# Latent attention: the normalised rows of tiles 2 to 15 are turned in 32x32 blocks by VectorE and put in order by DMA through DRAM, instead of by TensorE and ScalarE

## The chip, the cores and the metric

The kernel runs on one core of one Trainium2 chip. The metric is the device time of one execution in microseconds. Engines: PE is TensorE (PEld its weight loads), DVE is VectorE, ACT is ScalarE, POOL is GpSimd, SP is SyncE, which only issues DMAs (SPq is its queue).

## The reference

Two transformer layers over 64 sequences of 32 rows of 256 numbers: each is cross attention, self attention and a feed-forward part. The change lies in the cross attention of the second layer, over 257 context rows of 64 numbers, with 16 heads and keys kept in a latent form:

```python
x = x + _L1_xattn_ref(_layernorm(x, axis=-1), ctx_512, ...)
...
    q_hk = (hidden_q @ Wq.T).reshape(b, s, H, K)
    q_big = jnp.einsum('bshk,hkq->bshq', q_hk, w_kc_q)
    kv_rope = kv_c * cos[None] + _rotate_half(kv_c) * sin[None]
    q_r = jnp.einsum('bshq,hqr->bhsr', q_big, W_qr)
    k_r = jnp.einsum('bld,hdr->bhlr', kv_rope, W_kr)
    scores = jnp.einsum('bhsr,bhlr->bhsl', q_r, k_r)
    attn = jax.nn.softmax(scores, axis=-1)
    ctx_c = jnp.einsum('bhsl,bld->bhsd', attn, kv_rope)
    ctx_lat = jnp.einsum('bhsd,hkd->bshk', ctx_c, w_kc_kv)
    out = ctx_lat.reshape(b, s, H * K) @ Wo.T
```

Everything is in float32. The weights of the first and the last products are folded before this stage, so that one product gives the queries against `kv_rope` (`a_w`) and one gives the output (`b_w`).

## The kernel before

The 2048 rows are 16 tiles of 128 rows; a tile holds 4 sequences (TB) of 32 rows (SEQ). The stage is the function `latent_attention`. Each engine has its own program, and they meet by semaphores that count; every program walks the steps t = -2 to 16 (`run_steps`), and most steps are the two halves of a loop. In step t TensorE works on three tiles at once:

- `scores` of tile t, in 4 groups of 4 heads, each in one of two PSUM tiles `ps_s`, which is free again when ScalarE has taken the exponentials of the group before last in it
- `weigh_slots` and `weigh_tail`: the keys of tile t-1 weighed with its exponentials, and at the end `finish`, its output products
- `queries` of tile t+1 in two halves, from `xnT`, the normalised rows with their 256 columns on the partitions; then `last_key`, the scores of context row 257 of tile t+1
- `turn` of tile t+2: two transposes through PSUM that make `xnT`, which ScalarE copies out in `turned_out`

The order in a step of TensorE is: scores 0, weighing first half, scores 1, weighing second half and tail, scores 2, queries first half, scores 3, queries second half, output products, last key, turn. The first half of the weighing waits until VectorE has turned the last scores (`turn_last`, semaphore `last_ready`) and all exponentials of the tile.

VectorE takes in a step: inverse sums of tile t-1, then for the groups of tile t the maxima and, one group behind, the 32x32 transposes of the exponentials (`turn_exps`); between them it copies the weighed sums out; at the end it adds the residual, turns the last scores of the next tile, and takes the statistics of the finished row. ScalarE takes exponentials 0 and 1, a small copy, exponentials 2, the two copies of the queries (`queries_out`), exponentials 3 and the last exponentials, and then the copy of the turned row. SyncE loads keys (`load_kT`: two DMAs once the scores of tile t-2 are made, for tile t) and the inverse sums. GpSimd normalises the row of tile t+2 or t+3 (`row_normalised`) when the row before it has been turned, and multiplies the weighed sums by the inverses.

```python
                if live(1):
                    last_key(t + 1, 1 - u)
                if live(2):
                    turn(t + 2)
```

The DMAs of this kernel are issued by SyncE and GpSimd; ScalarE issues none.

Of the kernel before, what the change touches and what calls it, by code (L numbers as in the profile page):

```python
# [4 lines left out]
F32 = mybir.dt.float32  # L5
# [7 lines left out]
P = 128  # L13
# [1509 lines left out]
def latent_attention(nc, name, scope, moments, x_sb, consts, ident, latent_keys, last_roped, a_w, b_w, lastT, background=None):  # L1523
# [5 lines left out]
    xn = sb("xn", [P, DIM])  # L1529
    xnT = sb("xnT", [P, KC, P])  # L1530
    qT = [sb(f"qT{u}", [P, TB, pairs, SEQ]) for u in range(2)]
    kT, kv = latent_keys.kT, latent_keys.kv
# [23 lines left out]

    names = ("dve_next taken xn_ready turned xnT_ready q_made q_out cols_ready scores_made raw_top_ready top_ready "
             "exps_ready exps_turned last_made last_ready last_shifted last_exps whole_ready tail_filled tail_ready inverse_stored inverse_in0 inverse_in1 weighed "
# [4 lines left out]
    with nc.Block() as block:  # L1563
# [38 lines left out]
        def _(pool):  # L1602
# [14 lines left out]
            def row_normalised(t):  # L1617
                wait_count(pool, s["turned"], t)
                nc.gpsimd.tensor_scalar(xn[:, :], x_sb[:, t, :], moments.moments[:, t, 0:1], moments.factors[:, t:t + 1],
                                        ALU.subtract, ALU.mult).then_inc(s["xn_ready"], 1)  # L1620
# [11 lines left out]
        def _(pe):  # L1632
# [6 lines left out]
            def queries(t, part):  # L1639
                if part == 0:  # L1640
                    pe.wait_ge(s["xnT_ready"], t + 1)
                if isinstance(t, int) and t == 1:
                    pe.wait_ge(s["last_ready"], 1)
                wait_count(pe, s["sum_ready"], TB * (t - 2) + 1 + part)
                for n in range(4):
                    m = 4 * part + n
                    for c in range(KC):
                        last = nc.tensor.matmul(ps_q[part][:, n * P:(n + 1) * P], a_w[:, c, m * P:(m + 1) * P], xnT[:, c, :],  # L1648
                                                start=(c == 0), stop=(c == KC - 1))
                last.then_inc(s["q_made"], 1)  # L1650
# [64 lines left out]
            def step(t, u, live):  # L1715
                if live(0):
                    scores(t, u, 0)
                if live(-1):
                    if live(0):
                        pe.wait_ge(s["last_ready"], t + 1)  # L1720
                    if live(1):
                        pe.wait_ge(s["xnT_ready"], t + 2)
                    wait_count(pe, s["x_ready"], t - 1 if live(0) else t - 2)
# [40 lines left out]
                if live(1):  # L1764
                    last_key(t + 1, 1 - u)
                if live(2):
                    turn(t + 2)
# [5 lines left out]
        def _(act):  # L1773
# [25 lines left out]
            def queries_out(t, u, part):  # L1799
                act.wait_ge(s["q_made"], 2 * t + part + 1)  # L1800
                nc.scalar.copy(qT[u][:, :, 4 * part:4 * part + 4, :].rearrange("p b m q -> p m b q"),
                               ps_q[part][:, :].rearrange("p (m b q) -> p m b q", m=4, b=TB)).then_inc(s["q_out"], 1)

            def step(t, u, live):
                if live(0):
# [4 lines left out]
                if live(0):  # L1810
                    exponentials(t, u, 2)
                if live(1):
                    queries_out(t + 1, 1 - u, 0)
                    queries_out(t + 1, 1 - u, 1)
                if live(0):
                    exponentials(t, u, 3)
                    last_exponentials(t)
                if live(2):
                    turned_out(t + 2)
                if live(-1) and not live(0):  # L1820
                    act.wait_ge(s["inverse_made"], 1)
                    nc.scalar.copy(inverse[:, :, :].rearrange("p b n -> p (b n)"), ps_s[1][:, :]).then_inc(s["inverse_copied"], 1)
# [4 lines left out]
        def _(dve):  # L1827
            def normalise(t):
                wait_count(dve, s["turned"], t)
                moments.apply(t, row(x_sb, t), xn[:, :]).then_inc(s["xn_ready"], 1)  # L1830

            def maxima(t, u, g):
# [69 lines left out]
            def step(t, u, live):  # L1902
# [14 lines left out]
                if isinstance(t, int) and t < 0:  # L1917
                    normalise(t + 2)
                if live(0):
                    maxima(t, u, 3)  # L1920
# [954 lines left out]
```

## Time and profile before

| | |
|---|---|
| median of 3 runs | 1154.27 us (1152.2 to 1154.68) |
| profiled execution: time | 1154.21 us |
| profiled execution: span | 1152.4 us |
| busy over the span: PE, DVE, ACT, POOL | 1087.5, 708.1, 452.3, 301.6 us |
| the stage with the change | from 587 to 877 us of the span |
| mean DMA rate over the span | 72 GB/s |

Busy time is the time in which an engine has an instruction under way; of DMA issues the profile gives the time on the queue that issues them, and it doesn't count them as busy. Times in rows are microseconds from the start of the span, unless marked ns.

### The profile page before, as it was taken

What the parts mean: (1) busy time and instruction counts of PE and PEld (TensorE: products, weight loads), DVE (VectorE), ACT (ScalarE), POOL (GpSimd) and SP (SyncE); (2) the same over time, 40 slices, a digit from 0 to 9 for tenths busy, and PEclk for the clock granted to TensorE, in tenths of its full rate; (3) what the DMA queues carried; (4) which work ended last, traced back from release to release, by engine and by line L of the source; (5) the groups of instructions that cost most, each with busy time, mean ns of one, the idle gap of its engine ahead of it and who ended that gap; (6) DMA issues with size and microseconds to landing.
All of it is one profiled execution on the core that took longest, in us unless ns stands there. A gap on an engine that the chain in (4) does not pass through costs nothing. (4 is left out here: it accounts for less than half of the span.)

```text
span 1152.4 us, 32210 instructions
## 1 busy us (share of the span) xinstructions
PE 1087.5 (94%) x12466; PEld 830.2 (72%) x12467; DVE 708.1 (61%) x1806; ACT 452.3 (39%) x1329; POOL 301.6 (26%) x390
## 2 busy tenths in 40 slices
PE   7898999999999999999979999999998799899996
PEld 6676878888778768989756766776766588556664
DVE  6898754554646475646547888888885687422221
ACT  2453443434435222221145555555553565222221
POOL 1701523323131200000001221221214535234442
PEclk9899999999999999999989999999999998799998
DMA  8631211111121119000202323333244633312211
GB/s 266 173 89 36 71 46 49 43 39 55 27 55 27 37 35 253 1 0 0 57 1 70 92 75 78 77 84 76 70 139 145 200 77 100 84 30 35 35 27 11
DMA packets 72655, 82.56 MB, mean 72 GB/s; under 512 B 28942, under 2 KB 57263, under 8 KB 72140
## 3 DMA queue, kind: packets, MB, share of 16 engines
q1 hardware_dynamic: 64284, 62.33, 20.4%
q0 software_dynamic: 8304, 19.32, 6.4%
q8 instruction: 45, 0.74, 0.3%
q14 instruction: 22, 0.18, 0.1%
HBM read 64.91 MB, written 18.53 MB: 72 GB/s over the span
## 5 line engine op out<-in xcount | busy, mean ns | idle before, releaser
L1780 ACT ACTIVATE xattn_exps<-xattn_ps_s,xattn_top 128x256 f32<-128x256 f32 x256 | 117.8, 474 | 84.7 <-DVE xattn_top L1844 84.7
L777 PEld LDWEIGHTS attn_ps_q<-attn_xnT,w_b_q 128*128 128x128 f32 x1024 | 120.0, 194 | 12.6 <-issue 12.6
L777 PE MATMUL attn_ps_q<-attn_xnT,w_b_q 128*128 128x128 f32 x1024 | 124.6, 278 | 0.0
L831 PE MATMUL attn_ps_out<-w_b_o,attn_oT 128*128 128x256 f32 x480 | 106.6, 380 | 2.6 <-DVE all_x L1012 1.5
L831 PEld LDWEIGHTS attn_ps_out<-w_b_o,attn_oT 128*128 128x128 f32 x480 | 90.0, 190 | 16.1 <-DVE all_x L1012 2.4
L885 ACT COPY attn_qT<-attn_ps_q 128x512 f32<-128x512 f32 x64 | 38.1, 595 | 148.7 <-PE attn_ps_q L777 148.7
L1851 DVE STREAM_TRANSPOSE xattn_expsT<-xattn_exps 128x1024 f32<-128x1024 f32 x64 | 79.5, 1242 | 26.4 <-ACT xattn_exps L1780 26.3
L1841 DVE TENSOR_REDUCE xattn_raw_top<-xattn_ps_s 128x4 f32<-128x1024 f32 x64 | 77.3, 1208 | 14.7 <-PE xattn_ps_s L1671 14.2
L1648 PEld LDWEIGHTS xattn_ps_o<-xattn_xnT,all_d_a 128*128 128x128 f32 x512 | 61.9, 198 | 17.9 <-ACT xattn_exps L1780 7.2
L1613 POOL TENSOR_TENSOR xattn_ctxT<-xattn_weighed_sum,xattn_inverse 128x256 f32<-128x256 f32 x60 | 41.9, 730 | 125.3 <-DMA xattn_inverse<-xattn_inverse_rows 125.3
L1671 PE MATMUL xattn_ps_s<-all_c,xattn_qT 64*32 64x256 f32 x2048 | 69.8, 382 | 2.8 <-ACT xattn_exps L1780 2.8
L1648 PE MATMUL xattn_ps_o<-xattn_xnT,all_d_a 128*128 128x128 f32 x512 | 67.8, 288 | 4.1 <-ACT xattn_exps L1780 3.6
L1512 POOL TENSOR_TENSOR attn_k_halves<-attn_k_by_cos,attn_k_by_sin 128x256 f32<-128x256 f32 x32 | 23.5, 755 | 177.9 <-DVE attn_k_turned L1520 177.9
L1681 PE MATMUL xattn_ps_o<-xattn_expsT,all_c 32*64 32x256 f32 x2048 | 63.4, 380 | 1.6 <-DVE xattn_last_scores L1887 1.5
L963 DVE BATCH_NORM_STATS2 attn_out_stats<-attn_ps_out 128x6 f32<-128x256 f32 x15 | 6.5, 433 | 90.5 <-PE attn_ps_out L831 90.5
L1107 PE MATMUL ffn_ps_h<-ffn_xnT,all_c 128*128 128x128 f32 x512 | 61.1, 278 | 0.0
L1126 PE MATMUL ffn_ps_out<-all_c,ffn_masked 128*128 128x256 f32 x256 | 59.7, 380 | 0.0
L1107 PEld LDWEIGHTS ffn_ps_h<-ffn_xnT,all_c 128*128 128x128 f32 x512 | 58.5, 192 | 0.0
L1681 PEld LDWEIGHTS xattn_ps_o<-xattn_expsT,all_c 32*64 32x64 f32 x2048 | 43.1, 131 | 20.6 <-issue 11.0
L2603 DVE COPY all_d_b<-attn_ps_pT 128x512 f32<-128x512 f32 x23 | 15.9, 692 | 67.0 <-PE attn_ps_pT L2322 48.6
L1711 PE MATMUL xattn_ps_o<-all_d_b,xattn_ctxT 128*128 128x256 f32 x240 | 54.4, 380 | 1.6 <-DVE xattn_ctxT L1879 1.6
L1780 ACT ACTIVATION_READ_ACCUMULATOR xattn_exps<-xattn_ps_s,xattn_top 128x1 f32 x256 | 52.6, 206 | 0.0
(361 smaller groups left out, 2214.7 us busy)
## 6 DMA issues: line engine op xcount, KB each, us to landing
all_c<-roped_kT SPq DMA_DIRECT2D x32, 256.0 KB, 3.9
xattn_inverse<-xattn_inverse_rows SPq DMA_DIRECT2D x30, 256.0 KB, 4.0
attn_k_raw<-in_ctx SPq DMA_DIRECT2D x64, 64.0 KB, 1.9
roped_kv<-attn_k_kv SPq DMA_DIRECT2D x16, 256.0 KB, 2.1
roped_kT<-attn_k_turned SPq DMA_DIRECT2D x64, 64.0 KB, 1.7
all_c<-roped_kv SPq DMA_DIRECT2D x16, 256.0 KB, 2.9
moe_gate<-in_f_gate SPq DMA_DIRECT2D x8, 512.0 KB, 8.2
moe_up<-in_f_up POOLq DMA_DIRECT2D x8, 512.0 KB, 5.2
```

The lines of the kernel that those rows point to most:

```text
L777: last = nc.tensor.matmul(ps_q[g % 2][:, h * P:(h + 1) * P], wq[:, c, head * DH:(head + 1) * DH], xnT[u][:, c, :], start=(c == 0), stop=(c ...
L831: last = nc.tensor.matmul(bank[:, 0:DIM], of_heads[:, h, :, :].rearrange("p b q -> p (b q)"), wo[:, h, :], start=(h == 0), stop=(h == HEAD ...
L1107: last = nc.tensor.matmul(ps_h[half][:, j * P:(j + 1) * P], w1[:, c, f * P:(f + 1) * P], xnT[:, c, :], start=(c == 0), stop=(c == KC - 1))
L1126: last = nc.tensor.matmul(ps_out[:, 0:DIM], masked[u][:, f, :], w2[:, f, :], start=(f == 0), stop=(f == chunks - 1))
L1613: last = nc.gpsimd.tensor_tensor(ctxT[:, :, b, :], weighed_sum[:, :, b, :], inverse[:, b, :].rearrange("p (m q) -> p m q", q=SEQ), ALU.mult)
L1648: last = nc.tensor.matmul(ps_q[part][:, n * P:(n + 1) * P], a_w[:, c, m * P:(m + 1) * P], xnT[:, c, :], start=(c == 0), stop=(c == KC - 1))
L1671: last = nc.tensor.matmul(ps_s[g % 2][SEQ * b:SEQ * b + SEQ, 512 * odd + nkeys * n:512 * odd + nkeys * (n + 1)], qT[u][rows, b, 2 * g + n, :],
L1681: nc.tensor.matmul(ps_o[b][64 * odd:64 * odd + 64, 0:DIM], kv[u][rows, j, :], expsT[u][rows, :, odd, :, j, :], start=(j == 0), stop=False, ...
L1711: last = nc.tensor.matmul(out_bank(t), ctxT[:, m, :, :].rearrange("p b s -> p (b s)"), b_w[:, m, :], start=(m == 0), stop=(m == pairs - 1))
L1780: nc.scalar.activation(exps[g % 2][:, nkeys * k:nkeys * (k + 1)], ps_s[g % 2][:, nkeys * k:nkeys * (k + 1)], ACT.Exp, bias=top[u][:, n:n + ...
L1841: nc.vector.tensor_reduce(of_group(raw_top), ps_s[g % 2][:, :].rearrange("p (o m n) -> p o m n", o=2, m=2), X_AXIS, ALU.max, negate=True). ...
L1851: nc.vector.transpose(expsT[u][:, g, :, :, :, :].rearrange("p o m j q -> p (o m j q)"), exps[g % 2][:, :])\
```

## The change

Tiles 0 and 1 are turned as before, in the steps t = -2 and -1. For tiles 2 to 15 VectorE transposes the normalised row in 32x32 blocks into `xn_blocks`. ScalarE's queue then issues four DMAs, one for each group of 32 partitions, that write the blocks to a DRAM tensor in the order that a full transpose has (256 pieces of 128 bytes each, 1024 a tile), and, when all four have landed, one that reads it back into `xnT` (256 pieces of 512 bytes). GpSimd's wait for the row buffer and TensorE's wait for `xnT` follow.

```diff
+    xn_blocks = sb("xn_blocks", [P, DIM])
+    xnT_d = [nc.dram_tensor(f"{name}_xnT{u}", (KC, TB, SEQ, P), F32, kind="Internal").ap() for u in range(2)]
...
             def row_normalised(t):
-                wait_count(pool, s["turned"], t)
+                if t == 2:
+                    pool.wait_ge(s["turned"], 2)
+                else:
+                    pool.wait_ge(s["row_turned"], t - 2)
...
             def queries(t, part):
-                if part == 0:
+                if part == 0 and isinstance(t, int) and t < 2:
                     pe.wait_ge(s["xnT_ready"], t + 1)
+                elif part == 0:
+                    pe.wait_ge(s["xnT_in"], 16 * (t - 1))
...
-                    if live(1):
-                        pe.wait_ge(s["xnT_ready"], t + 2)
...
-                if live(2):
+                if isinstance(t, int) and t < 0:
                     turn(t + 2)
...
+            def rows_out(t, u):
+                act.wait_ge(s["row_turned"], t - 1)
+                for b in range(TB):
+                    nc.scalar.dma_start(xnT_d[u][:, :, :, SEQ * b:SEQ * b + SEQ].rearrange("c k d j -> d (c k) j"),
+                                        xn_blocks[SEQ * b:SEQ * b + SEQ, :].rearrange("d (n j) -> d n j", j=SEQ)).then_inc(s["row_out"], 16)
+
+            def rows_in(t, u):
+                act.wait_ge(s["row_out"], 64 * (t - 1))
+                nc.scalar.dma_start(xnT[:, :, :], xnT_d[u].rearrange("c k d n -> (k d) c n")).then_inc(s["xnT_in"], 16)
...
                 if live(1):
+                    if live(0) and live(2):
+                        rows_out(t + 2, u)
                     queries_out(t + 1, 1 - u, 0)
                     queries_out(t + 1, 1 - u, 1)
                 if live(0):
                     exponentials(t, u, 3)
                     last_exponentials(t)
-                if live(2):
+                if isinstance(t, int) and t < 0:
                     turned_out(t + 2)
+                elif live(2):
+                    rows_in(t + 2, u)
...
+            def turn_row(t):
+                dve.wait_ge(s["xn_ready"], t + 1)
+                wait_count(dve, s["row_out"], 64 * (t - 2))
+                nc.vector.transpose(xn_blocks[:, :], xn[:, :]).then_inc(s["row_turned"], 1)
...
                 if isinstance(t, int) and t < 0:
                     normalise(t + 2)
+                elif live(2):
+                    turn_row(t + 2)
```

In ScalarE's program this is the second part of a loop half before the change, from exponentials 2 (`xattn_exps`) on; the copies of the queries are `xattn_qT`:

```order
L1780 ACTIVATE xattn_exps,xattn_total<-xattn_ps_s,xattn_top 128x256 x4
L1800 ISA
L1801 COPY xattn_qT<-xattn_ps_o 128x4x4x32
L1800 REGISTER_ALU
L1801 COPY xattn_qT<-xattn_ps_o 128x4x4x32
L1777 REGISTER_ALU
L1780 ACTIVATE xattn_exps,xattn_total<-xattn_ps_s,xattn_top 128x256 x4
L1787 ACTIVATE xattn_tail<-xattn_last_shifted 128x16
L1790 REGISTER_ALU
L1791 COPY xattn_xnT<-xattn_ps_o 128x256
```

The same place in the changed kernel:

```order
L1785 ACTIVATE xattn_exps,xattn_total<-xattn_ps_s,xattn_top 128x256 x4
L1812 DMA xattn_xnT<-xattn_xn_blocks 32x8x32 x4
L1805 ISA
L1806 COPY xattn_qT<-xattn_ps_o 128x4x4x32
L1805 REGISTER_ALU
L1806 COPY xattn_qT<-xattn_ps_o 128x4x4x32
L1782 REGISTER_ALU
L1785 ACTIVATE xattn_exps,xattn_total<-xattn_ps_s,xattn_top 128x256 x4
L1792 ACTIVATE xattn_tail<-xattn_last_shifted 128x16
L1816 REGISTER_ALU
L1817 DMA xattn_xnT<-xattn_xnT 128x2x128
```

Four DMA issues now stand between exponentials 2 and the copies of the queries, and a fifth stands at the end, where the copy of the turned row was.

In TensorE's program this is the end of a loop half before the change, from the last output product (`xattn_ctxT`) to the weighing of the next step (`xattn_expsT`):

```order
L1711 MATMUL xattn_ps_o<-all_d_b,xattn_ctxT 128x256
L1656 MATMUL xattn_ps_o<-xattn_qT,xattn_last_cols 32x256 x8
L1634 REGISTER_ALU
L1636 MATMUL xattn_ps_o<-all_consts,xattn_xn 128x128 x2
L1671 MATMUL xattn_ps_s<-all_c,xattn_qT 32x256 x16
L1725 ISA
L1681 MATMUL xattn_ps_o<-xattn_expsT,all_c 64x256 x32
```

In the changed kernel the L1634 and L1636 rows are gone and the scores follow the last key.

In VectorE's program of the changed kernel the new transpose (`xattn_xn_blocks`) stands between the turn of exponentials 1 (`xattn_expsT`) and the maxima of group 3 (`xattn_raw_top`):

```order
L1875 STREAM_TRANSPOSE xattn_expsT<-xattn_exps 128x1024
L1852 REGISTER_ALU
L221 REGISTER_ALU
L1854 STREAM_TRANSPOSE xattn_xn_blocks<-xattn_xn 128x256
L1864 REGISTER_ALU
L1865 TENSOR_REDUCE xattn_raw_top<-xattn_ps_s 128x2x2
```

Before, the maxima followed the turn of exponentials 1 directly.

## Rows read from the trace of the kernel before

**Rows 1.** Busy time of each engine (instructions), clock, DMA share, GB/s, the stage.

```profile
600.00:877.00 277.00, 268.23 (x5318) 189.76 (x5318) 226.17 (x419) 146.47 (x585) 57.78 (x73) 1.00 0.31 85
```

**Rows 2.** Timeline of a step: start, us, engine, line, operation, idle before and releaser.

```profile
714.39 1.98 PE L1681 MATMUL xattn_ps_o<-xattn_expsT,all_c 32*64 32x256 f32 x64
...
721.98 2.79 POOL L1613 TENSOR_TENSOR xattn_ctxT<-xattn_weighed_sum,xattn_inverse 128x256 f32<-128x256 f32 x4 [7.21 <-DMA xattn_inverse<-xattn_inverse_rows]
...
722.68 1.25 DVE L1851 STREAM_TRANSPOSE xattn_expsT<-xattn_exps 128x1024 f32<-128x1024 f32 x1
...
724.02 2.05 PE L1648 MATMUL xattn_ps_o<-xattn_xnT,all_d_a 128*128 128x128 f32 x16
...
724.20 1.22 DVE L1841 TENSOR_REDUCE xattn_raw_top<-xattn_ps_s 128x4 f32<-128x1024 f32 x1 [0.27 <-PE xattn_ps_s L1671]
724.33 1.19 SPq L1437 DMA_DIRECT2D all_c<-roped_kT  x2
...
724.59 0.60 ACT L1801 COPY xattn_qT<-xattn_ps_o 128x512 f32<-128x512 f32 x1
...
725.91 3.62 PE L1711 MATMUL xattn_ps_o<-all_d_b,xattn_ctxT 128*128 128x256 f32 x16
726.11 0.58 ACT L1801 COPY xattn_qT<-xattn_ps_o 128x512 f32<-128x512 f32 x1 [0.92 <-PE xattn_ps_o L1648]
726.59 0.48 ACT L1780 ACTIVATE xattn_exps<-xattn_ps_s,xattn_top 128x256 f32<-128x256 f32 x1
...
728.56 1.25 DVE L1851 STREAM_TRANSPOSE xattn_expsT<-xattn_exps 128x1024 f32<-128x1024 f32 x1 [1.69 <-ACT xattn_exps L1780]
...
729.46 0.66 PE L1656 MATMUL xattn_ps_o<-xattn_qT,xattn_last_cols 64*32 64x256 f32 x16
729.73 0.38 DVE L1892 TENSOR_TENSOR all_x<-all_x,xattn_ps_o 128x256 f32 x1
...
730.05 0.44 PE L1636 MATMUL xattn_ps_o<-all_consts,xattn_xn 128*128 128x128 f32 x2
730.23 0.78 DVE L1887 STREAM_TRANSPOSE xattn_last_scores<-xattn_ps_o 128x256 f32<-128x256 f32 x2
...
730.53 0.37 ACT L1791 COPY xattn_xnT<-xattn_ps_o 128x256 f32<-128x256 f32 x1 [1.89 <-PE xattn_ps_o L1636]
...
731.45 1.98 PE L1681 MATMUL xattn_ps_o<-xattn_expsT,all_c 32*64 32x256 f32 x64
...
733.83 0.47 ACT L1780 ACTIVATE xattn_exps<-xattn_ps_s,xattn_top 128x256 f32<-128x256 f32 x1 [2.92 <-DVE xattn_top L1844]
```

**Rows 3.** Waits of ScalarE, 600 to 877 us: total, times, longest.

```profile
ACT xattn_qT L1801 <- PE xattn_ps_o L1648: 11.0, 15, 1.9
```

**Rows 4.** Timeline of the boundary to the last tile, where no row is turned.

```profile
848.50 0.66 PE L1656 MATMUL xattn_ps_o<-xattn_qT,xattn_last_cols 64*32 64x256 f32 x16
...
849.27 0.78 DVE L1887 STREAM_TRANSPOSE xattn_last_scores<-xattn_ps_o 128x256 f32<-128x256 f32 x2
...
850.10 1.53 PEld L1681 LDWEIGHTS xattn_ps_o<-xattn_expsT,all_c 32*64 32x64 f32 x64 [0.56 <-DVE xattn_last_scores L1887]
```

**Rows 5.** SyncE's issues: one timeline row, then ns min/median/max by tile.

```profile
139.04 1.77 SPq L1482 DMA_DIRECT2D roped_kT<-attn_k_turned  x4
...
L2053 SPq DMA_DIRECT2D attn_v_blocks<-attn_v_stage x64: 302/426/1382, 888.4 to 969.0; - x64
...
L1584 SPq DMA_DIRECT2D xattn_inverse<-xattn_inverse_rows x30: 593/626/1079, 615.1 to 853.9; - x30
...
L1576 SPq DMA_DIRECT2D xattn_kv_last<-last_roped x64: 227/232/290, 586.5 to 840.4; - x64
```

**Rows 6.** DMA from 940 to 960 us: packets, share of 16 engines, landing.

```profile
DMA packets 3120, 0.76 MB, mean 38 GB/s; under 512 B 3120, under 2 KB 3120, under 8 KB 3120
...
q1 hardware_dynamic: 3120, 0.76, 20.6%
...
attn_v_blocks<-attn_v_stage SPq DMA_DIRECT2D x18, 34.0 KB, 1.9
```

More of the change, by code:

```diff
@@ L1555, in latent_attention @@
     batches = (2, 3, 0, 1)
-    names = ("dve_next taken xn_ready turned xnT_ready q_made q_out cols_ready scores_made raw_top_ready top_ready "
+    names = ("dve_next taken xn_ready turned xnT_ready row_turned row_out xnT_in q_made q_out cols_ready scores_made raw_top_ready top_ready "
              "exps_ready exps_turned last_made last_ready last_shifted last_exps whole_ready tail_filled tail_ready inverse_stored inverse_in0 inverse_in1 weighed "
```

## The prediction

> **What bounds the kernel now.** I first read the stage's stretch from the windows: 277 us in which TensorE is busy 268 us, VectorE 226, ScalarE 146 and the 16 DMA engines 31% [rows 1]. By shares alone TensorE is the bound, and work taken off it should pay. So I looked next at how one step ends, since the 16 steps are almost alike and one is 17.06 us long (weighing starts at 714.39 and again at 731.45) [rows 2].
>
> The timeline of one step's end shows two paths that run side by side and arrive together [rows 2]. Path one is TensorE itself: second half of the queries from 724.02, output products from 725.91, last key at 729.46, the turn of the row at 730.05, then the scores of group 0, and weighing at 731.45, with hardly a gap. Path two leaves TensorE when the queries are made: ScalarE copies them out at 726.11, having stood idle 0.92 us for them, takes exponentials of group 3 from 726.59, VectorE turns those from 728.56 (idle 1.69 for ScalarE), adds the residual at 729.73, and turns the last scores from 730.23 to 731.01. Weighing waits for that (last_ready). It starts 0.44 us after it. So VectorE's path has less than half a microsecond of slack against TensorE's, and behind it stands ScalarE, whose only slack between the exponentials of group 2 and those of group 3 is that wait for the queries. The waits give it for the whole stage: 11.0 us in 15 times, 0.73 us each [rows 3]. That 0.73 is the number that decides here. ScalarE's low busy share says nothing of it: its large idle time lies at the start of a step, before the exponentials of group 0 at 733.83 [rows 2].
>
> **What the change takes away.** TensorE no longer makes the two transposes of 730.05. What that is worth is seen in the trace itself, since the boundary to the last tile already has no turn [rows 4]: there the last key starts at 848.50 and weighing at 850.10, 1.60 us later, against 1.99 us with the turn (729.46 to 731.45). That is 0.39 us, less than the 0.44 us which the transposes show, because weighing then stands 0.56 us for VectorE's last scores and starts 0.05 us after they end. So I book -0.39 us a step, the most that can come: after it the bound at this place is path two. ScalarE's copy of 0.37 us at 730.53 goes too; it lay in idle time and I book nothing, and if that cover were gone it would be worth its 0.37 us.
>
> **What it adds to VectorE.** One transpose of 128x256 between the turn of exponentials 1 and the maxima of group 3. The nearest row is the last scores' pair at 730.23, 0.78 us for two of that size, so 0.4 us. Maxima 3 start at 724.20 and would start at about 724.4 (the transpose before them ends at 723.93); exponentials of group 3 wait for the queries' copy until 726.59, so this lies under ScalarE's wait. Without that cover it would cost 0.4 us. It adds two waits to VectorE's queue, with maxima 3 behind them: for the row itself, and for the four transfers of the tile before, which were issued 17 us earlier. GpSimd normalises a row as soon as the row before is turned; that comes now at 724.4, and in its queue stands behind its four products (721.98 to 724.77), so it follows them, a whole step ahead of need. The products must be done before the output products at 725.91; they stay ahead of the moved work and keep their 1.1 us [rows 2].
>
> **What it adds to ScalarE.** Per step four DMA issues on its own queue, between the exponentials of group 2 and the first copy of the queries, in front of both copies and of the exponentials of group 3; and one more at the step's end. ScalarE issues no DMA in the kernel before, so the price is bounded from SyncE's [rows 5]. Four issues in a row of 32 partitions into DRAM took 1.77 us; the 32x4x68 ones 302 ns at least and 426 in the median; the 64x4x256 one, with as many pieces (256) as each new DMA has, 626 ns; a single row 232 ns. I take 1.77 us for the four, since these have the same 32 partitions on the source side, and keep 4 x 0.302 = 1.21 and 4 x 0.626 = 2.50 as ends. They start when VectorE's new transpose has ended (723.93 + 0.4) and exponentials 2 are done (724.6), so at about 724.6. SyncE issues its two loads of keys at 724.33 for 1.19 us, at the same moment. Nothing in the trace shows two such queues issuing at once, so the extra is between nothing and 1.19 us; I take half of one key issue (1.19 / 2 / 2), 0.30 us, because ScalarE meets at most the rest of one if they alternate. The 1024 new packets of 128 bytes a step do not gate anything: packets of 272 bytes cost 3120 in 20.6% of 16 x 20 us, 21 ns each [rows 6], so 64 on an engine are 1.4 us, and SyncE's keys, which share the engines then, belong to the tile after next. The landing is some 2 us after the last issue, before ScalarE is done with exponentials 3 (728.5 plus the delay) and reaches the fifth issue. That one (0.3 to 0.63 us) lies in the idle stretch before 733.83, and its data has until the queries of the next step, behind weighing and two groups of scores; TensorE's new wait there, with the queries and the last two groups of scores behind it, is met.
>
> **The sum.** Per step 1.77 + 0.30 - 0.73 (ScalarE's slack) - 0.39 (what TensorE gives back before weighing) = 0.95 us slower. What is late next is exponentials 3, then VectorE's turn of them, the residual, the last scores, and with them weighing and every later step of the cycle; nothing in a step recovers it, since maxima 1 follow the scores that are issued behind weighing. Fourteen tiles (2 to 15) are moved, in steps 0 to 13: 14 x 0.95 = 13.3 us. The profiled execution took 1154.21 us (its span is 1152.4 and some 1.8 lie around it), the median of three is 1154.27, so they are one number here. 1154.2 + 13.3 = **1167.5 us**. Ends of the known terms: (1.21 - 1.12) x 14 = 1 us, giving 1155.5; (2.50 + 1.19 - 1.12) x 14 = 36 us, giving 1190.
>
> **Rivals.** (1) *Faster: the issues hide in the wait for the queries.* The change wins where four issues take under 1.12 us, 0.28 us each; the single-row issue of 232 ns is under that, the lowest of the 32-partition ones is not. At 0.232 us it gives (0.93 - 1.12) x 14 = -2.7 us, and if all of it were hidden 14 x -0.39 = -5.5 us: 1149 to 1151. For it speaks also that ScalarE's queue could issue while its exponentials still run. Against: the issues wait for row_turned, which comes only some 0.2 us before these end. Chance 0.12. (2) *No change*, between these: 0.06, 1154.
>
> (3) *SyncE's key issues hold ScalarE's in full*: 1.77 + 1.19 - 1.12 = 1.84 a step, 26 us, **1180**. For it: the two start within 0.3 us of each other in every step, and both hang on the same scores. Against: no row shows two queues slowing each other. Chance 0.12. The Trainium skill, Perfetto Trace Analysis, section on the HWDGE DMA instruction, says that the sequencer locks one shared descriptor generator and that this wait is inside the profiled time of an issue. No row here can show it for ScalarE; by this rule the time would be that of rival 3.
>
> (4) *The round trip is late.* The fifth issue waits until all 1024 small packets have landed, and behind it on ScalarE are the next step's exponentials. From the first issue at 724.6 to 733.83 there are 9 us; it decides when a 128-byte packet costs over some 0.11 us (64 of them and 1.9 us of landing), five times the 21 ns of rows 6. At 0.15 us the wait is 2.5 us more a step, 35 us on top: about 1202. Chance 0.10. The Trainium skill, DMA: Bandwidth & Descriptors, Specifications, says that a transfer under 512 bytes is done as read-modify-write; packets of 272 bytes in rows 6 show no such price, and no run yet shows 128 bytes written in scattered pieces.
>
> The likeliest has 0.60. **Chances**: a measurement of this kernel can tell about 0.2%, 2.3 us, from no change; faster 0.12, within 0.07, slower 0.81. The range that leaves out rival 1 and most of rival 4 goes from 1154.5 to 1187; the likeliest alone would be 1157 to 1177.
>
> **What would show it.** In the changed kernel's timeline: four issues on ScalarE's queue after the exponentials of group 2, their sum (1.77 us?), the idle time before its copies of the queries gone, exponentials 3 of a step later after their scores, weighing waiting for the last scores (as in rows 4) in every step, TensorE with idle time of about 1.4 us more a step, a step of 18.0 us instead of 17.06. The issues' length beside SyncE's at the same moment tells rival 3; a wait of the fifth issue past the next maxima tells rival 4. I am wrong if an issue on ScalarE is far from SyncE's price, either way.

## The result, and the profile after

| | before | after |
|---|---|---|
| median (runs) | 1153.96 us (6; 1152.2 to 1157.48) | 1163.76 us (6; 1159.09 to 1168.86) |
| profiled execution: time, span | 1154.21, 1152.4 us | 1162.11, 1160.3 us |
| the stage, from the first activation of the cross attention to the first of the self attention behind it | 290.2 us | 303.2 us |
| mean step in the stage (14 distances between SyncE's first inverse-sum issues) | 17.01 us | 17.89 us |

The ratio is 1.0083 [1.0055, 1.0112]: slower, by 9.8 us. Forecast were 1167.5 us, +13.3.

The windows view of the stage after (columns as in [rows 1]); the same work now takes about 13 us longer, and TensorE is busy less in it:

```profile
600.00:890.00 290.00, 264.80 (x5291) 189.58 (x5276) 228.49 (x432) 140.11 (x567) 57.95 (x74) 0.99 0.36 94
```

The timeline of one step after, to be laid beside [rows 2] (weighing begins at 720.91 here, at 714.39 there):

```profile
720.91 1.99 PE L1688 MATMUL xattn_ps_o<-xattn_expsT,all_c 32*64 32x256 f32 x64 [1.37 <-DVE xattn_last_scores L1911]
...
728.88 2.80 POOL L1615 TENSOR_TENSOR xattn_ctxT<-xattn_weighed_sum,xattn_inverse 128x256 f32<-128x256 f32 x4 [14.06 <-DMA xattn_inverse<-xattn_inverse_rows]
...
730.71 0.40 DVE L1854 STREAM_TRANSPOSE xattn_xn_blocks<-xattn_xn 128x256 f32<-128x256 f32 x1
...
730.95 1.20 SPq L1437 DMA_DIRECT2D all_c<-roped_kT  x2
731.02 0.48 ACT L1785 ACTIVATE xattn_exps<-xattn_ps_s,xattn_top 128x256 f32<-128x256 f32 x1
731.03 1.18 DVE L1865 TENSOR_REDUCE xattn_raw_top<-xattn_ps_s 128x4 f32<-128x1024 f32 x1
731.13 0.36 ACTq L1812 DMA_DIRECT2D xattn_xnT<-xattn_xn_blocks  x1
...
731.53 1.55 ACTq L1812 DMA_DIRECT2D xattn_xnT<-xattn_xn_blocks  x3
731.65 1.23 POOL L1624 TENSOR_SCALAR xattn_xn<-all_x,all_moments,all_moments_work 128x256 f32<-128x256 f32 x1
...
733.19 1.07 ACT L1806 COPY xattn_qT<-xattn_ps_o 128x512 f32<-128x512 f32 x2 [1.61 <-PE xattn_ps_o L1655]
...
734.15 0.49 ACT L1785 ACTIVATE xattn_exps<-xattn_ps_s,xattn_top 128x256 f32<-128x256 f32 x1
...
736.13 1.25 DVE L1875 STREAM_TRANSPOSE xattn_expsT<-xattn_exps 128x1024 f32<-128x1024 f32 x1 [2.47 <-ACT xattn_exps L1785]
736.22 0.38 ACTq L1817 DMA_DIRECT2D xattn_xnT<-xattn_xnT  x1
...
737.61 0.76 DVE L1911 STREAM_TRANSPOSE xattn_last_scores<-xattn_ps_o 128x256 f32<-128x256 f32 x2
...
738.50 0.67 PE L1688 MATMUL xattn_ps_o<-xattn_expsT,all_c 32*64 32x256 f32 x13 [0.90 <-DVE xattn_last_scores L1911]
```

Read it from the issues. The four take from 731.13 to 733.08. The first starts while the last exponential of group 2 (731.02 to 731.50) still runs, 0.37 us before its end. What it waited for is the row: VectorE's transpose ends at 731.11 and the issue starts at 731.13, and it follows the transpose by no more than 0.04 us in every step of the loop. Then ScalarE does no work until the copies of the queries at 733.19. The view calls this 1.61 us of waiting for TensorE; but TensorE had made the first half long before, and the copies follow the last issue by 0.11 us: the issues held them. Exponentials 3 come 13.24 us after weighing began (before: 726.59 - 714.39 = 12.20), so 1.04 us later. Not all of that is the issues' doing. The exponentials of group 2 ended 10.59 us after weighing began here and 10.23 in the step of [rows 2]; this time varies between 10.2 and 10.8 us in the usual steps of both kernels, and before the change the wait for the queries evened it out. From exponentials 3 to the next weighing it is 4.35 us (before 4.86), so 0.51 us of the delay is taken up, and this step is 17.59 us long instead of 17.06. The waits of the stage after (total, times, longest) show it in all steps:

```profile
ACT xattn_qT L1806 <- PE xattn_ps_o L1655: 24.7, 14, 2.8
...
PE xattn_ps_o L1688 <- DVE xattn_last_scores L1911: 17.3, 14, 2.0
```

ScalarE stands 1.76 us a step where it stood 0.73 [rows 3], and TensorE now waits for the last scores in every step, 1.24 us each, as at the boundary of [rows 4]. The issues themselves, from the tile's view (ns min/median/max), and the transposes:

```profile
L1812 ACTq DMA_DIRECT2D xattn_xnT<-xattn_xn_blocks x56: 309/472/1562, 603.9 to 839.2; - x56
L1854 DVE STREAM_TRANSPOSE xattn_xn_blocks<-xattn_xn x14: 396/398/404, 603.5 to 837.2; 128x256 f32<-128x256 f32 x14
```

The 14 distances are 19.59, 17.73, 18.44, 17.78, 17.63, 17.76, 17.79, 17.75, 17.64, 17.76, 18.14, 17.75, 17.53, 17.23 us. The usual distance is 17.75; the first is an outlier. Counted from one start of weighing to the next, most steps in TensorE's loop alternate instead, near 17.95 in one half and 17.45 to 17.6 in the other (before: 16.98 and 17.06); the mean over both halves is the same either way. The windows view of the first (columns as in [rows 1]):

```profile
610.00:612.00 2.00, 0.04 (x6) 0.00 (x0) 1.88 (x4) 0.20 (x2) 0.00 (x0) 1.00 0.23 69
612.00:614.00 2.00, 1.92 (x48) 1.56 (x56) 1.93 (x5) 0.00 (x0) 0.00 (x0) 0.67 0.01 5
614.00:616.00 2.00, 2.00 (x43) 0.84 (x36) 0.40 (x2) 1.54 (x7) 0.00 (x0) 0.50 0.04 12
616.00:618.00 2.00, 2.00 (x74) 1.31 (x66) 1.16 (x1) 0.39 (x2) 0.00 (x0) 0.98 0.78 196
```

and TensorE's timeline there:

```profile
608.51 0.67 PE L1663 MATMUL xattn_ps_o<-xattn_qT,xattn_last_cols 64*32 64x256 f32 x16 [1.82 <-ACT xattn_qT L1806]
...
612.08 3.24 PE L1688 MATMUL xattn_ps_o<-xattn_expsT,all_c 32*64 32x256 f32 x64 [2.04 <-DVE xattn_last_scores L1911]
615.25 1.46 PE L1678 MATMUL xattn_ps_s<-all_c,xattn_qT 64*32 64x256 f32 x32
```

Here the issues took 0.35 + 2.80 us. TensorE stood 1.82 us, worked 1.5, stood 2.04, and then the granted clock fell from 1.00 to 0.50 (1.2 of 2.4 GHz) for about 3 us: weighing took 3.24 us for 1.99, the scores 1.46 for 1.09, 1.6 us lost on top of the delay. Around the gap of 1.37 us at 720.91 (first line of the step above) it stayed at 1.00.

### The profile page after: what moved, and what is told of

Its sections match the earlier page's. It is cut to its first block and busy times, and to the rows that moved or that the text cites. A ratio compares the mean times of both kernels' runs of the same rounds, so it can differ in the third digit from the quotient of the medians.

```text
span 1160.3 us, 32232 instructions
## 1 busy us (share of the span) xinstructions
PE 1081.9 (93%) x12438; PEld 828.3 (71%) x12439; DVE 709.6 (61%) x1820; ACT 446.9 (39%) x1315; POOL 301.3 (26%) x390
## 3 DMA queue, kind: packets, MB, share of 16 engines
q10 hardware_dynamic: 19040, 3.67, 1.8%
## 5 line engine op out<-in xcount | busy, mean ns | idle before, releaser
L1678 PEld LDWEIGHTS xattn_ps_s<-all_c,xattn_qT 64*32 64x32 f32 x2048 | 33.7, 106 | 27.9 <-issue 13.7
```

Source lines behind the costliest of these rows:

```text
L1678: last = nc.tensor.matmul(ps_s[g % 2][SEQ * b:SEQ * b + SEQ, 512 * odd + nkeys * n:512 * odd + nkeys * (n + 1)], qT[u][rows, b, 2 * g + n, :],
```

## The experiments

The ratios are against the kernel before, run beside each group of kernels. Its median in these groups was 1149.59 to 1153.96 us, so medians of different rows are compared by their ratios only. The step is the mean of the same 14 distances. Where an interval holds 1, the kernel can't be told from the one before.

| | median us | ratio | step us | stage us |
|---|---|---|---|---|
| changed kernel | 1163.76 | 1.0083 [1.0055, 1.0112] | 17.89 | 303.2 |
| issues on SyncE | 1148.79 | 0.9967 [0.9944, 0.9990] | 16.88 | 288.5 |
| no transfers | 1148.46 | 0.9978 [0.9952, 1.0005] | 16.86 | 290.1 |
| turn kept | 1160.99 | 1.0079 [1.0049, 1.0109] | 17.71 | 299.1 |
| issues at the end | 1149.53 | 0.9982 [0.9954, 1.0010] | 16.89 | 288.5 |
| one out, four in | 1149.21 | 0.9974 [0.9941, 1.0006] | 16.90 | 288.3 |
| eight issues | 1197.89 | 1.0411 [1.0362, 1.0460] | 20.42 | 340.0 |
| keys later | 1158.40 | 1.0059 [1.0036, 1.0083] | 17.64 | 298.9 |
| SyncE, statistics moved | 1147.03 | 0.9959 [0.9930, 0.9988] | 16.82 | 286.5 |
| two ahead, two at the end | 1147.99 | 0.9981 [0.9960, 1.0002] | 16.87 | 288.6 |
| three ahead, one at the end | 1151.67 | 1.0020 [0.9997, 1.0043] | 17.21 | 292.0 |

**Where does the time hang: on the issues, the transfers or the turn?** Three kernels. In the first the same five DMAs are issued by SyncE, after its other loads of the step:

```diff
-                    nc.scalar.dma_start(xnT_d[u][:, :, :, SEQ * b:...
+                    if b == TB - 1:
+                        sp.wait_ge(s["q_made"], 2 * t)
+                    nc.sync.dma_start(xnT_d[u][:, :, :, SEQ * b:...
```

> All five DMAs of a row are issued by SyncE, behind its loads of keys, and none by ScalarE; the transpose on VectorE, the traffic and the absence of the turn on TensorE stay as in the changed kernel. Theory (issue time on ScalarE ahead of the queries' copies is the whole loss): the loss of 9.8 us goes and what the missing turn gives stays, 14 x -0.39 us, so about 1148.5 us, 5 below the kernel before. Rival (the loss comes from the new traffic, from VectorE's transpose or from GpSimd's moved row): stays near 1163.

In the second VectorE's transpose stays and all five DMAs go, with the waits for them, so TensorE's queries use an old row:

```diff
-                    pe.wait_ge(s["xnT_in"], 16 * (t - 1))
...
-                        rows_out(t + 2, u)
...
-                    rows_in(t + 2, u)
```

> The five DMAs are left out, so the queries of tiles 2 to 15 use the normalised row of tile 1; VectorE's transpose stays, TensorE doesn't turn. Theory: no issue ahead of the queries' copies, so as e1: 1148 to 1149 us. If the traffic itself costs, this one is faster than e1 by that cost. If VectorE's transpose or GpSimd's moved row costs, both stay above 1149.

In the third all of the change stays, and TensorE's turn and ScalarE's copy of it come back; the fifth DMA fills a tile that nobody reads:

```diff
-                if isinstance(t, int) and t < 0:
+                if live(2):
                     turn(t + 2)
...
-                nc.scalar.dma_start(xnT[:, :, :], ...
+                nc.scalar.dma_start(xnT_unused[:, :, :], ...
```

> As the changed kernel, but TensorE also turns the rows and ScalarE copies them out as before, and the queries use these; the fifth DMA writes to a tile that nobody reads. Theory: while ScalarE's issues make the path over exponentials 3 and the last scores the late one, TensorE's turn lies in its waiting time, so the turn costs under 1 us in all: about 1164 us, the same as the changed kernel. Rival (removing the turn still brings its 0.39 us in each of 14 steps, and the issues cost that much more): 1169 us.

Measured: issues on SyncE 0.9967, no transfers 0.9978, turn kept 1.0079. With the issues off ScalarE the loss is gone, and taking the transfers away altogether brings no more (steps 16.88 and 16.86): the packets and the round trip cost nothing that can be seen here; what costs is the issues on ScalarE. And with the turn kept the kernel is as slow as the changed one, in steps of 17.75 again: the turn's removal gives nothing there. Its timeline, at the end of a step, has the two transposes back (699.62), and the weighing starts after the last scores all the same:

```profile
693.76 0.31 ACTq L1814 DMA_DIRECT2D xattn_xnT<-xattn_xn_blocks  x1
...
694.10 1.79 ACTq L1814 DMA_DIRECT2D xattn_xnT<-xattn_xn_blocks  x3
...
699.62 0.44 PE L1641 MATMUL xattn_ps_o<-all_consts,xattn_xn 128*128 128x128 f32 x2
...
701.32 1.99 PE L1688 MATMUL xattn_ps_o<-xattn_expsT,all_c 32*64 32x256 f32 x64 [0.24 <-DVE xattn_last_scores L1913]
```

**The same issues at another place on ScalarE.** `rows_out(t + 2, u)` moves from ahead of the copies of the queries to just ahead of `rows_in`, behind the last exponentials:

```diff
-                    if live(0) and live(2):
-                        rows_out(t + 2, u)
...
                 elif live(2):
+                    rows_out(t + 2, u)
                     rows_in(t + 2, u)
```

> ScalarE issues the four DMAs at the end of its step, behind exponentials 3 and the last exponentials, right before the fifth, in the idle stretch of some 5 us. Theory (only their place ahead of the queries' copies costs): 1149 us if all lands before the next maxima are ready; the fifth issue's wait for the landing (3.6 us in the changed kernel's trace, beside 1.9 us of issues) may hold the next exponentials 0 by up to 0.8 us a step, so up to 1158 us. Rival (ScalarE's issues cost wherever they stand): 1163 us.

Measured 0.9982, step 16.89. ScalarE's rows of one step of this kernel, with the VectorE row that its last activation waits for and the next weighing:

```profile
724.54 0.58 ACT L1806 COPY xattn_qT<-xattn_ps_o 128x512 f32<-128x512 f32 x1 [1.02 <-PE xattn_ps_o L1655]
...
725.16 0.14 DVE L1879 TENSOR_TENSOR xattn_last_shifted<-xattn_last_scores,xattn_top 128x16 f32<-128x16 f32 x1
...
725.34 0.31 ACTq L1812 DMA_DIRECT2D xattn_xnT<-xattn_xn_blocks  x1
...
725.68 0.80 ACTq L1812 DMA_DIRECT2D xattn_xnT<-xattn_xn_blocks  x1
...
726.51 0.56 ACTq L1812 DMA_DIRECT2D xattn_xnT<-xattn_xn_blocks  x1
...
726.83 0.25 ACT L1792 ACTIVATE xattn_tail<-xattn_last_shifted 128x16 f32<-128x16 f32 x1
...
727.09 0.47 ACTq L1812 DMA_DIRECT2D xattn_xnT<-xattn_xn_blocks  x1
...
728.80 0.38 ACTq L1817 DMA_DIRECT2D xattn_xnT<-xattn_xnT  x1
...
729.57 1.99 PE L1688 MATMUL xattn_ps_o<-xattn_expsT,all_c 32*64 32x256 f32 x64 [0.16 <-DVE xattn_last_scores L1910]
```

Four issues of 2.14 us in all, on the same queue, and they cost nothing: they stand behind the exponentials in the program, and no work of ScalarE is behind them until the next step. The first three start while ScalarE's activations, which the program has ahead of them, are still under way (exponentials 3 from 725.02, the last exponentials to 727.08); the fourth starts at 727.09, as those end. The first starts 0.04 us after VectorE has made what the last activation waits for (725.16 + 0.14), 1.74 us before that activation ends. So what an issue waits for on ScalarE's queue is, by the rows of both kernels, the last semaphore that it or an instruction ahead of it waits for, and not the end of those instructions.

**One DMA out, four back.** The order is made on the way back in; only one issue stands ahead of the copies, four at the end:

```diff
-                for b in range(TB):
-                    nc.scalar.dma_start(xnT_d[u][:, :, :, SEQ * b:SEQ * b + SEQ]...
+                nc.scalar.dma_start(xnT_d[u], xn_blocks[:, :]).then_inc(s["row_out"], 16)
...
+                for k in range(TB):
+                    nc.scalar.dma_start(xnT[SEQ * k:SEQ * k + SEQ, :, :]...
```

> ScalarE writes the turned blocks to DRAM as they are, with one issue ahead of the queries' copies, and puts them in order when it reads them back, with four issues of 256 pieces of 128 bytes at the end of its step. The same five issues on the same engine, only one of them ahead of the copies. Theory: one issue of 0.31 us is less than ScalarE's wait for the queries, so steps are as in the run with SyncE's issues (16.9 us), about 1150 us. Rival (five issues on ScalarE cost what they cost, wherever): 1163 us.

Measured 0.9974, step 16.90: as with none ahead. The one issue takes 0.34 us in the median.

**Eight issues ahead.** The four are issued once more, first into a tensor that nobody reads:

```diff
+                for b in (0, 1, 2, 3):
+                    nc.scalar.dma_start(unused_d[u][:, :, :, SEQ * b:SEQ * b + SEQ]...
```

> The changed kernel with four more issues of the same form ahead of the queries' copies, to a DRAM tensor that nobody reads. Theory: nothing is left to hide them, so each costs its whole length: 4 x 0.47 = 1.9 us a step, steps of 19.7 us instead of 17.75, 14 x 1.9 = 26 us more, about 1190 us. Rival (the loss is a wait that doubling the issues doesn't double, as for data to land): under 1175 us.

Measured 1.0411. ScalarE and TensorE in one step of it:

```profile
708.98 0.36 ACTq L1813 DMA_DIRECT2D xattn_unused<-xattn_xn_blocks  x1
...
709.37 1.47 ACTq L1813 DMA_DIRECT2D xattn_unused<-xattn_xn_blocks  x3
...
710.87 2.34 ACTq L1816 DMA_DIRECT2D xattn_xnT<-xattn_xn_blocks  x4
713.33 1.07 ACT L1807 COPY xattn_qT<-xattn_ps_o 128x512 f32<-128x512 f32 x2 [3.89 <-issue]
...
714.54 0.69 PE L1719 MATMUL xattn_ps_o<-all_d_b,xattn_ctxT 128*128 128x256 f32 x2 [0.96 <-ACT xattn_qT L1807]
...
718.64 3.33 PE L1689 MATMUL xattn_ps_o<-xattn_expsT,all_c 32*64 32x256 f32 x64 [1.95 <-DVE xattn_last_scores L1915]
```

The second four take 2.34 us, more than the 1.9 that was expected, and the usual step grows from 17.75 to 20.2, 2.45 us: all of it arrives. That is why the time is 1197.89 us and not 1190, together with three of the 14 steps that are 21.7 us and more. In the one shown weighing takes 3.33 us, with the granted clock at 0.50 from 720 to 722 us. The gaps ahead of it are the 0.96 and 1.95 us in the rows; but most steps of this kernel have such a pair (1.01 and 1.94, 1.64 and 2.05), and in those weighing takes 1.99 us. What makes the clock fall in three of them is not settled.

**Keys later.** SyncE's two key loads wait until the queries are made, so that they no longer meet the first issues:

```diff
-                sp.wait_ge(s["scores_made"], groups * (t - 1))
+                sp.wait_ge(s["q_made"], 2 * t)
```

> The changed kernel, but SyncE issues its two loads of keys when the second half of the queries is made, some 1.8 us later, so that they don't meet ScalarE's four issues. Theory with a shared descriptor generator (0.3 us a step booked for the meeting): the four issues fall from 2.1 us to about 1.75, steps from 17.75 to 17.4 us, 5 us in all, about 1158.5. Rival (two queues don't slow each other): issues and time as in the changed kernel, 1163.

Measured 1158.40 us, 1.0059 [1.0036, 1.0083]. Its interval overlaps with the changed kernel's, so the time alone does not show the gain; the rows of both queues and the steps do:

```profile
729.53 0.31 ACTq L1812 DMA_DIRECT2D xattn_xnT<-xattn_xn_blocks  x1
...
729.88 1.47 ACTq L1812 DMA_DIRECT2D xattn_xnT<-xattn_xn_blocks  x3
...
731.47 1.07 ACT L1806 COPY xattn_qT<-xattn_ps_o 128x512 f32<-128x512 f32 x2 [1.48 <-PE xattn_ps_o L1655]
...
731.47 1.19 SPq L1437 DMA_DIRECT2D all_c<-roped_kT  x2
```

Alone, the four take 1.82 us from the first start to the last end; in the changed kernel, beside SyncE, 1.95 in the step shown, 1.86 to 2.27 in the ten usual steps and 2.12 in their mean. The usual step is 17.33 to 17.47 instead of 17.75.

**SyncE's issues, and VectorE's statistics moved.** The statistics of the finished row (0.42 us) move from a step's end to ahead of the last turn of exponentials in the next step:

```diff
+                    if live(-2):
+                        statistics(t - 2)
                     turn_exps(t, u, 3)
...
-                if live(-1):
+                if isinstance(t, int) and t == TILES - 1:
                     statistics(t - 1)
```

> The kernel with all five issues on SyncE, and VectorE's statistics of the finished row (0.42 us and a small memset) moved out of the chain last scores, inverse sums, maxima 0, exponentials 0, copies of the weighed sums, into VectorE's idle time before the turn of exponentials 3. Theory: without the turn on TensorE this chain is what the steps wait for (16.87 us instead of the 17.02 - 0.39 that was forecast), so steps fall to about 16.6 us and the time by another 3 to 4 us, to 1145. Rival (something else holds the step, such as exponentials 1): as the kernel with SyncE's issues, 1149.

Measured 0.9959 [0.9930, 0.9988], the lowest ratio here, but its interval overlaps with that of the issues on SyncE alone (0.9967 [0.9944, 0.9990]), so no gain over it is shown. The reason given was wrong: the first two distances are 16.61, but then they alternate between 16.68 and 17.05 as with the issues on SyncE alone, and from weighing to weighing the steps of the loop are 16.85 to 16.90 us in both kernels. The statistics held none of them. What does is answered in part further on, under rival 1.

**Two or three issues ahead.** Of the four, two (three) stay ahead of the copies, the others stand beside the fifth:

```diff
-                        rows_out(t + 2, u)
+                        rows_out(t + 2, u, range(2))
...
+                    rows_out(t + 2, u, range(2, TB))
                     rows_in(t + 2, u)
```

> Two of the four issues stay between exponentials 2 and the copies of the queries, the other two stand with the fifth at the step's end; nothing is left out. Theory (what the four issues cost is what exceeds 0.36 us of queue run-ahead and 0.73 us of waiting for the queries): two issues are 1.03 us by the 2.07 us of the four, under 1.09, so they cost nothing: steps of 16.9 us as with none there, about 1149.5 us. Rival (every issue there costs its own length, and the changed kernel's step is 17.75 for four and 16.88 for none, a straight line): 17.3 us steps, 1149.5 + 0.43 x 14 = 1155.6 us.

> Three of the four issues stay between exponentials 2 and the copies of the queries, one stands with the fifth at the step's end; nothing is left out. Theory: three issues are 1.55 us, 0.46 over the 1.09 us of cover; exponentials 3 come 0.46 us later, of which the later path's slack against TensorE (0.39 us, since the turn is gone) takes most: steps of 16.9 to 17.2 us, 1150 to 1154 us. Rival (a straight line from none to four): 17.53 us steps, 1149.5 + 0.65 x 14 = 1158.6 us.

Measured: two 0.9981, step 16.87; three 1.0020, step 17.21. A straight line is out: none and two ahead cost the same, the third 0.34 us a step, the fourth 0.68, each of four more 0.63, in the mean. The third costs in one half of TensorE's loop alone. Weighing starts of the kernel with three:

```profile
715.09 1.99 PE L1688 MATMUL xattn_ps_o<-xattn_expsT,all_c 32*64 32x256 f32 x64 [0.82 <-DVE xattn_last_scores L1912]
...
731.94 1.99 PE L1688 MATMUL xattn_ps_o<-xattn_expsT,all_c 32*64 32x256 f32 x64 [0.15 <-DVE xattn_last_scores L1912]
...
749.42 1.96 PE L1688 MATMUL xattn_ps_o<-xattn_expsT,all_c 32*64 32x256 f32 x60 [0.84 <-DVE xattn_last_scores L1912]
```

The steps are 16.85 and 17.48 us; with two ahead they are 16.85 and 16.87. With two, ScalarE's rows of one step show where they fit:

```profile
724.61 0.31 ACTq L1812 DMA_DIRECT2D xattn_xnT<-xattn_xn_blocks  x1
...
724.96 0.47 ACTq L1812 DMA_DIRECT2D xattn_xnT<-xattn_xn_blocks  x1
...
725.54 0.59 ACT L1806 COPY xattn_qT<-xattn_ps_o 128x512 f32<-128x512 f32 x1 [0.50 <-issue]
726.53 0.59 ACT L1806 COPY xattn_qT<-xattn_ps_o 128x512 f32<-128x512 f32 x1 [0.41 <-PE xattn_ps_o L1655]
```

The second copy still waits 0.41 us for TensorE's second half: in this step the wait for the queries had not been used up. In the steps of the other half it had been, and exponentials 3 come 0.1 to 0.2 us later there, but the step is no longer for it.

**The kernel before once more.**

> The kernel before once more, with a profile. If the last stage (from 877 us on) of the first profiled execution was a slow one, this execution's is nearer 270 us than 275, with steps of 17.0 us in the stage as then; if 275 us belong to the kernel, it is there again.

Its steps are the same (mean 17.02, stage 290.7 us), and what follows the stage took 265.8 us, against 274.7 in the first profiled execution and 270.7 in the changed kernel's. So the 274.7 do not belong to the kernel, and whole spans of single executions say little here; the stage of a trace does (290.2 and 290.7 before, 303.2 after), and the medians.

## Why the prediction was right, and where its sum was not

The sign and the mechanism held: issues between exponentials 2 and the copies of the queries use up ScalarE's wait for the queries and then push exponentials 3, the last scores and the weighing. The forecast was +13.3 us; the stage of the traces gives 303.2 - 290.2 = +13.0, the medians +9.8 (6.3 to 12.9 by the interval). That the stage comes so near is in part luck: the forecast was 14 equal steps of +0.95, and what came is usual steps of +0.75 and three long ones. The figures of usual steps below are means over nine steps from weighing to weighing, those that start between 660 and 810 us in each trace. Term by term:

- **Four issues, 1.77 us.** 1.78 where nothing meets them (0.31 + 1.47, keys later). SyncE's row of the same 32 partitions was the right neighbour.
- **Meeting SyncE, 0.30 us.** 2.12 us beside SyncE and 1.82 without it are 0.30 in the mean (0.04 to 0.45 in single steps), and the step is 0.3 to 0.4 shorter when the keys are moved away. The forecast took it from an argument, half of one issue, and there is luck in so close a hit. Rival 3's full 1.19 us is refuted: SyncE's two issues take 0.54 to 0.55 us each with and without ScalarE's in all usual steps, and ScalarE's four lost a quarter of their sum. The page that the rival names (the Trainium skill, Perfetto Trace Analysis, section on the HWDGE DMA instruction) puts a wait for the shared generator inside an issue's profiled time; the trace agrees in that some of ScalarE's issues take 0.6 to 0.7 us there instead of 0.47. But issues of the two queues overlap in the rows for most of their length, so one does not wait for the whole of the other.
- **Slack for the queries, -0.73 us.** It held (0.70 in usual steps): a kernel with two issues there is no slower than one with none.
- **What was missing: the start ahead of the exponentials' end.** The first issue starts 0.35 us before the exponentials of group 2 end, so that much is hidden. The prediction named this in rival 1, with the right cause (the issues wait for the row to be turned, some 0.2 us before that end) and near the right size, and then left it out of the sum. So this is no bound on how far the queue can run ahead, as it is called where two or three issues are forecast: with the issues at the end it is 1.74 us. Also missing are 0.12 us from the last issue to the copies.
- **"What TensorE gives back before weighing", -0.39 us.** This is the step that failed in its reason. Kept or removed, the turn makes no difference that shows here (1.0079 and 1.0083; usual steps 17.74 and 17.77). What took up part of the delay was the other path's own slack, the 0.44 us by which the last scores had been ready before the weighing; it would have been there without the change to TensorE. When path two becomes the bound, work taken off TensorE is worth nothing, and one of the two had to be booked, not the turn. Its size was near: from exponentials 3 to weighing the time fell from 4.85 to 4.43 us, 0.42.

The sum for a usual step as the runs have it: 2.12 (the four issues beside SyncE's) + 0.12 - 0.35 - 0.70 - 0.42 = 0.77 us, and the usual step grew by 0.75 (17.77 against 17.02). 14 x 0.75 = 10.5 us; about the rest of the 13 us in the trace's stage are the distances of 19.59, 18.44 and 18.14 (2.9 us over 17.75 together). Of these only the third (18.44) has a pattern: the third distance is also 18.2 to 18.4 with the turn kept, with the keys later and with three ahead, and SyncE's second key issue in that step is long in the kernel before as well (1.14 us for 0.54). The first is 17.95 with the turn kept and 19.18 with the keys later. Whether the runs outside the profiler have such a first step cannot be seen; their +9.8 would fit 14 usual ones.

**Rival 1** lost, but its point was right: it put the balance at 1.12 us of issues. Two (0.8 to 1.0 us) leave the small gain there is, three (1.3 to 1.6 us) give it back, four (1.86 and more) lose. The full gain it promised, -0.39 a step, does not come either: with the issues out of the way the mean step falls only by 0.12 (17.01 to 16.89), to about 1149 us. From weighing to weighing one can see why. With the issues at the end two steps that lead to a weighing outside TensorE's loop (from 611.59 and from 797.05) are 16.61 us, and that is the full gain; those that lead to one in the loop are 16.85 to 16.88, but for one of 17.07. There weighing waits for the last scores, as in the changed kernel, but starts 0.13 us after them in one half of the loop and 0.32 in the other, where it is 0.06 at the end of the two steps of 16.61. In the first of these halves TensorE has also waited 0.35 us for VectorE's weighed sums ahead of the queries, which puts exponentials 3 off by 0.17. Why weighing starts later in the loop is not settled.

**Rival 4** lost clearly. From the view of DMAs (packets, MB, share; median landing) in the stage after:

```profile
q10 hardware_dynamic: 19040, 3.67, 7.1%
...
xattn_xnT<-xattn_xn_blocks ACTq DMA_DIRECT2D x56, 32.0 KB, 3.6
xattn_xnT<-xattn_xnT ACTq DMA_DIRECT2D x14, 128.0 KB, 2.2
```

That is 0.071 x 16 x 290 us / 19040 = 17 ns a packet, in the mean of the pieces written and those read back, below the 21 ns of [rows 6]; the Trainium skill (DMA: Bandwidth & Descriptors, Specifications) has transfers under 512 bytes done as read-modify-write, and a price for that does not show. They land in 3.6 us, not 2. Here too it is the meeting with the keys and not the small pieces: the same four DMAs land in 1.8 us at the end of the step and in 1.7 with the keys later. The fifth issue is held by them: in the step shown it starts at 736.22, and the last of the four has landed 0.02 us before; so it is in every step. That costs nothing, since ScalarE's next exponentials come only some 5 us later, so the rival had the right wait and the wrong price.

**VectorE and GpSimd** did as said: the transpose took 0.40 us, maxima 3 followed it at 731.03 without a wait; GpSimd's products ended at about 731.7, ahead of the output products at 732.53, and the row came behind the products.

## What to carry to other kernels

Before a DMA issue is put on a compute engine's queue, read what stands behind it there: its length counts only beyond that engine's next wait, so the same four issues cost 1.0% at one place (1.0083 against 0.9982) and nothing 2.4 us later in the step (12.62 us after weighing began instead of 10.22). An issue ahead of an engine's work can start as soon as its semaphores allow, so look also for when its data is ready: here each bit of time by which VectorE's transpose came before the end of exponentials 2 was hidden. Where two paths meet, a delay on one is cut by the slack between them, and work removed from the other gains nothing; book the one or the other, and test by keeping the removed work. Count the gaps that a delay makes in TensorE, too: around some of the long ones, not all, the clock fell on top.

## What the runs showed of the hardware

- ScalarE's queue issues DMAs while its earlier activations still run: 0.37 us ahead of the end of exponentials 2 (0.02 us after the transpose that the issue waits for), and 1.74 us ahead of the end of the last exponentials in the kernel with the issues at the end, where three of four start before that end. Their price shows only when work stands behind them.
- An issue of 32 partitions in 256 pieces takes ScalarE's queue 0.31 us for the first and 0.47 to 0.49 for those behind it; the 128x2x128 read back takes 0.38.
- Two queues that issue together cost one of them 0.30 us in four issues (mean; 0.04 to 0.45) and the other nothing in the usual steps; the four transfers land in 3.6 us instead of 1.7 to 1.8.
- The granted clock fell to 0.50 for some 3 us after gaps of 1.82 and 2.04 us with 1.5 us of work between them, and not after the single gap of 1.37 us in the step shown (1.00 from 720 to 724 us). With eight issues ahead it fell in three of 14 steps and not in others with the same gaps.
